# An attention kernel on one core: a transpose and a wait moved one slot on, and a pair of loads set apart

## The chip, the cores and the metric

One core of a Trainium2 chip. TensorE (PE) multiplies matrices, VectorE (DVE) and ScalarE (ACT) work on rows of 128 partitions, GpSimd (POOL) does the same more slowly, and SyncE (SP) here only issues transfers (DMAs). Each engine runs its own list of instructions in order, and semaphores join the lists. The metric is the time of one run on the device, in microseconds (us).

## What is computed

Two layers on 8 batches of 112 query rows and 375 context keys, all in float32, width 512. The first is an attention block with 16 heads of width 32 and an MLP. The second has two cross-attentions (called passes here) over the same context, each with 16 heads of width 128 and one learned extra key and value, and then an MLP:

```python
qh = (q_in @ wq + bq).reshape(b, q_len, H, K)
kh = (kv_in @ wk + bk).reshape(b, t, H, K)
vh = (kv_in @ wv + bv).reshape(b, t, H, K)
kh = jnp.concatenate([kh, bias_k], axis=1)   # broadcast over the batch
vh = jnp.concatenate([vh, bias_v], axis=1)
logits = jnp.einsum('bqhk,bthk->bhqt', qh, kh) / scale
weights = jax.nn.softmax(logits, axis=-1)
ctx = jnp.einsum('bhqt,bthk->bqhk', weights, vh).reshape(b, q_len, H * K)
x = res + ctx @ wo + bo
```

## The kernel before, in words

A float32 value is kept as two halves, high and low, and a product of two matrices is three matrix multiplications (high by high, high by low, low by high; `product`, L1877).

The two passes of the second layer take most of the run, and the change lies in them alone (`attend(a)` of each engine, a = 0 and 1). A pass works through 4 groups of 4 heads. For each group it walks over the 8 batches, so a pass has 32 places, each a (group, batch) pair. The batches of a group are called first to eighth below (`place.b` 0 to 7). Each place has 4 **slots**, t = 0 to 3, one for each head of its group. The place of a group is unrolled, and every engine's list is written by the same loop over places and slots, so that the order of the work is fixed by the code.

What the slots of a place hold, engine by engine:

- PE, in every slot: the keys of the head three ahead (`key`, 12 multiplications into `ps_k` or `ps_t`), then a part of the context sum of the place before (`context_sum`, 9 multiplications, probabilities `pt` by context `ckd`, into `ps_v` or `ps_o`), then the scores of the head two ahead (`scores`, 3 multiplications into `ps_s`). In the second and sixth batch (not in the second of a pass's first group) slots 2 and 3 hold no context sum but the output of two heads each for the four batches before (`head_output`, from `sums` and `w_b`); the place after takes twice the context sums in its slots 0 and 1.
- ACT: the high halves (`k_hi`, `sums_hi`), the exponentials (`prob`), and once a place, in slot 0, the high half of the turned probabilities (`pt_hi`, L1216).
- DVE: the low halves (`k_lo` L1642, `sums_lo` L1677), the maximum of each row (L1648), the scaling of the probabilities (L1536), and for each head one transposition of 32x32 squares (L1666) that writes the probabilities into the one buffer `blocks`.
- POOL: the low half of the turned probabilities (`pt_lo`, L944, three products of 1.3 us) in slot 1.
- SP issues, in this order: in slot 0 the context halves `cs_hi` and `cs_lo` of the place two ahead (`load_halves`, L641), when the keys of this place are done; in slot 1 the queries `q` of the place two ahead (L691), when this place's last scores are done; in slot 2 the store of `blocks` to the DRAM tensor `turned_probabilities` (L750), when all four heads of the place are in it; in slot 3 its load back as `pt_lo` in four pieces (L760), when the store has landed. Between them stand the loads of `ckd` (L651), and in the fourth and fifth batch of groups two to four the weights of the next group (`w_raw_a`, `w_raw_b`, 1 MB a batch). All are on one queue, SP's.

Since DVE works two heads ahead, the first head of a place is turned in slot 2 of the place before, and has to wait there until the store of `blocks` (L750) has read the buffer and landed (`blocks_out`, L1665). The turned probabilities then go store, load, `pt_hi`, `pt_lo`, and are used by PE in slot 2 of the next place (of the first and fifth batch: two places on).

Of the kernel before, what the change touches and what calls it, by code (L numbers as in the profile page):

```python
# [190 lines left out]
def build(nc, x_in, ctx_in, kd_in_all, mask_in, blocks_a, blocks_b, vec_a, vec_b, value_rows, value_bias_rows, row_bias, eye, out):  # L191
# [7 lines left out]
    with ExitStack() as ctx:  # L199
# [401 lines left out]
        def _(sp):  # L601
# [36 lines left out]
                    dst = ctx_scr[ds(place.b, 1), s].rearrange("o p f -> (o p) f")  # L638
                    sp.dma_start(dst, cs[place.parity][s][:, 0:DT * KW].bitcast(F32)).then_inc(ctx_out[place.parity], 16)

            def load_halves(place):  # L641

                for s in range(2):
                    src = ctx_scr[ds(place.b, 1), s].rearrange("o p f -> (o p) f")
                    sp.dma_start(cs[place.parity][s][:, 0:DT * KW].bitcast(F32), src).then_inc(ct_in[place.parity], 16)

# [76 lines left out]
            def attend(a):  # L723
                def store_head(place, t):
                    sp.wait_ge(z_ev, NT * place.quads + t + 1)
                    sp.sem_inc(sp_waited, 1)
                    b0 = place.b - place.quarter
                    dst = o_scr[place.group, b0:b0 + 4, :, t * LQ:(t + 1) * LQ].rearrange("b p r -> p b r")
                    sp.dma_start(dst, o_head[t % 2]).then_inc(z_out[t % 2], 16)

                def store_extra(place):
                    sp.wait_ge(extra_ev, NT * place.visit + NT)
                    sp.sem_inc(sp_waited, 1)
                    dst = pex_scr[ds(place.block, 1), ds(place.b, 1)].rearrange("o b (r t) -> r (o b t)", t=NT)
                    sp.dma_start(dst, extra_p[:, NT * place.parity:NT * place.parity + NT]).then_inc(extra_out[place.parity], 16)

                def load_extra(place):
                    first = place.quarter - 2
                    for i in range(2):
                        sp.wait_ge(extra_out[i], 16 * (place.pairs + first))  # L740
                    wait(sp, z_term, NT * place.quads)
                    sp.sem_inc(sp_waited, 1)
                    src = pex_scr[ds(place.block, 1), ds(place.b - 2 + first, 2)].rearrange("o b f -> o (b f)")
                    sp.dma_start(extra[:, 2 * first * NT * P:(2 * first + 2) * NT * P],
                                 src.partition_broadcast(P)).then_inc(extra_in, 16)

                def store_blocks(place):
                    sp.wait_ge(block_turn, turned_heads(place, NT))
                    sp.sem_inc(sp_waited, 1)
                    sp.dma_start(turned_scr[place.parity], image(place)).then_inc(blocks_out, 16)  # L750

                def load_turned(place):
                    sp.wait_ge(blocks_out, 16 * turned_batches(place) + 16)
                    wait(sp, c_mm, NT * (place.visit - 1))
                    sp.sem_inc(sp_waited, 1)
                    src = turned_scr[place.parity].rearrange("(i a) (s f) -> s a i f", i=BANDS, s=4)
                    for s in range(4):
                        rows = slice(SQUARE * s, SQUARE * (s + 1))
                        dst = pt[place.parity][1][rows, :].bitcast(F32).rearrange("a (i f) -> a i f", i=BANDS)
                        sp.dma_start(dst, src[s]).then_inc(turned_in[place.parity], 16)  # L760

                def q_stored(group):
                    for i in range(4):
                        sp.wait_ge(q_out[i], 16 * stores_before(i, 1, a, group))
                    sp.sem_inc(sp_waited, 1)

                def prologue(place):
                    def between(i):
                        if i == 0:
                            q_stored(1)  # L770
                            load_q(place)
                            load_q(place.next())

                    last_query(query, a, between, FIRST_PIECES)

                def all_queries_stored():
                    for i in range(4):
                        sp.wait_ge(q_out[i], 16 * stores_before(i, 1, a + 1, 0))
                    sp.sem_inc(sp_waited, 1)

                def one_batch(place):
                    for t in range(NT):
                        if t == 0 and place.after(2):
                            sp.wait_ge(k_mm, place.tile + NT)
                            sp.sem_inc(sp_waited, 1)
                            load_halves(place.after(2))
                        if t == 0 and place.final:
                            sp.wait_ge(k_mm, place.tile)
                            land(0, a, (0, 1))
                        if t == 1 and place.after(2):  # L790
                            load_q(place.after(2))
                        if t == 2:
                            store_extra(place)
                            if not place.final:
                                store_blocks(place)
                        if t == 3:
                            if not place.final:
                                load_turned(place)
                            if place.quarter >= 2:
                                load_extra(place)  # L800
                        for head in heads(place, t):
                            store_head(quad_before(place), head)
                        for summed, d in chunks(place, t):
                            load_by_key(summed.next(), d)
                        if query_piece(place, t):
                            last_query(query, a, skip, query_piece(place, t))
                        if place.fetches is not None:
                            load_block(place.fetches, (place.block_a, place.block_b)[place.fetches] + 1, [t])
                    if place.head and place.parity == 0:
                        all_queries_stored()  # L810

                def epilogue(place):
                    sp.wait_ge(k_mm, place.tile + NT)
                    sp.sem_inc(sp_waited, 1)
                    land(0, a, (2,))
                    load_block(0, place.block_a + 2)
                    for t in range(NT):
                        store_head(place, t)

                batches(sp, a, prologue, one_batch, epilogue)  # L820
# [574 lines left out]
        def _(dve):  # L1395
# [243 lines left out]
            def attend(a):  # L1639
# [11 lines left out]
                def normalized_1(place, t):  # L1651
# [6 lines left out]
                                          ALU.mult).then_inc(extra_ev, 1)  # L1658

                    normalize(place.unit + t, prob[buf], buf, extra_probability, slice(0, P))  # L1660
                    if place.final:
                        return
                    dve.wait_ge(s_norm, place.unit + t + 1)
                    if t == 0:
                        wait(dve, blocks_out, 16 * (turned_batches(place) - (place.head and place.parity)))  # L1665
# [24 lines left out]
                def prologue(place):  # L1690
                    def between(t):
                        if t == 0:
                            split_q(place)
                            key_lo(place, 0)
                            key_lo(place, 1)
                            maximum(place, 0)
                        if t == 1:
                            normalized_1(place, 0)
                            key_lo(place, 2)
                            maximum(place, 1)  # L1700
                            normalized_1(place, 1)

                    last_query(query, a, between, FIRST_PIECES)

                def one_batch(place):
                    for t in range(NT):
# [3 lines left out]
                            key_lo(*place.key(t + 3))  # L1710
                        for head in heads(place, t)[1:2]:
                            output(quad_before(place), head)
                        if place.final:
                            for summed, d in chunks(place, t):
                                sum_lo(summed, d)
# [8 lines left out]
                        for summed, d in () if place.final else chunks(place, t)[-1:]:  # L1724
                            sum_lo(summed, d)
                        if place.key(t + 2):
                            normalized_1(*place.key(t + 2))
                        if query_piece(place, t):
                            last_query(query, a, skip, query_piece(place, t))
                        if t == 0 and not place.final:  # L1730
# [145 lines left out]
        def _(pe):  # L1876
# [180 lines left out]
            def attend(a):  # L2057
# [55 lines left out]
                def one_batch(place):  # L2113
                    for t in range(NT):
                        for head in heads(place, t)[0:1]:
                            head_output(quad_before(place), head)
                        if t == 2 and not place.final:
                            pe.wait_ge(q_lo, place.batch + 2)
                        if place.key(t + 3):
                            key(*place.key(t + 3))  # L2120
                        for head in heads(place, t)[1:2]:
# [2 lines left out]
                            last_query(query, a, skip, query_piece(place, t))  # L2124
                        if t > 1 and query_piece(place, 3):
                            last_piece(place, t)
                        for summed, d in chunks(place, t):
                            context_sum(summed, d)
                            if place.final and t == 2 and d < 2:
                                last_turned(place, d + 2)  # L2130
# [151 lines left out]
```

## Time and profile before

| | |
|---|---|
| median of 3 runs | 2285.13 us (2279.72 to 2288.86) |
| the profiled execution's own time | 2283.49 us |
| its span, first to last instruction | 2281.6 us, granted PE clock 0.998 |
| PE busy | 2222.9 us (97%), 12347 matrix multiplications |
| DVE, ACT, POOL busy | 60%, 49%, 28% |
| SP's queue | 477.7 MB, 65.9% of 16 DMA engines' span |

The page says that PE is nearly always busy, so a change can win at most the little idle time that PE has, and can lose as much as it makes PE wait. In a row of the time line, the bracket at the end gives the engine's idle time just before the instruction, and what ended it. The window view gives, for each engine, busy time and number of instructions, and then the granted clock of PE, the share of time in which the DMA engines were busy, and what they moved.

### The profile page before, as it was taken

How to read it: one execution, taken by the hardware profiler on the slowest of the kernel's cores; microseconds unless marked ns; L12 is line 12 of the kernel's file. 1: busy time of each engine (PE TensorE's matmuls, PEld its weight loads, DVE VectorE, ACT ScalarE, POOL GpSimd, SP SyncE). 2: the span in 40 equal slices, each digit the busy share in tenths (PEclk: the TensorE clock that was granted, in tenths of full speed). 3: DMA queues.
4: the chain of work that ended last, by engine and by line, in shares of the span. 5: the costliest groups of instructions: out<-in, count | busy, mean ns of one | idle time of the engine just before them, and what ended most of it. 6: DMA issues, size and time to landing. Idle time of an engine off the chain costs nothing.

```text
span 2281.6 us, 36274 instructions
## 1 busy us (share of the span) xinstructions
PE 2222.9 (97%) x12347; PEld 2005.4 (88%) x12347; DVE 1376.4 (60%) x3070; ACT 1120.4 (49%) x2282; POOL 647.0 (28%) x945
## 2 busy tenths in 40 slices
PE   7999999999999999999999999999999999999999
PEld 6777788888999899899888898999899899888888
DVE  6877774524666666666654616666666566554743
ACT  5777753344455454455453434555455455453421
POOL 2111055421232332232322212233233133133421
PEclk9999999999999999999999999999999999999999
DMA  5422136566988888988975557987988988864110
GB/s 190 147 91 104 57 100 201 171 234 193 293 255 280 276 272 258 285 271 260 299 217 151 200 170 239 291 271 243 293 273 254 277 282 262 269 211 137 52 54 33
DMA packets 327767, 480.04 MB, mean 210 GB/s; under 512 B 65822, under 2 KB 250034, under 8 KB 327586
## 3 DMA queue, kind: packets, MB, share of 16 engines
q1 hardware_dynamic: 327586, 477.73, 65.9%
q8 instruction: 101, 1.65, 0.3%
q14 instruction: 80, 0.66, 0.1%
HBM read 368.72 MB, written 108.92 MB: 209 GB/s over the span
## 4 chain that ended last, share of the span: by engine, by line
PE 78%; DMA 8%; DVE 5%; issue 3%; SPq 3%; ACT 2%; POOL 1%; DVEq 0%; ACTq 0%; POOLq 0%
PE ps_o L1880 7%; PE ps_o L1882 7%; PE ps_o L1881 7%; PE ps_v L1880 5%; PE ps_k L1880 5%; PE ps_k L1881 5%; PE ps_k L1882 5%; PE ps_v L1882 5%; PE ps_v L1881 5%; DMA turned_probabilities<-blocks 5%; PE ps_t L1881 4%; PE ps_t L1882 4%; PE ps_t L1880 4%; PE ps_s L1880 4%; PE ps_s L1882 3%; PE ps_s L1881 3%
## 5 line engine op out<-in xcount | busy, mean ns | idle before, releaser
L944 POOL TENSOR_TENSOR pt_lo<-pt_lo,pt_hi 128x512 fp32r<-128x512 f32 x186 | 243.1, 1334 | 201.0 <-ACT pt_hi L1216 201.0
L1251 ACT ACTIVATE prob<-ps_s,row_columns 128x376 f32<-128x376 f32 x256 | 147.1, 575 | 249.9 <-DVE row_columns L1648 248.1
L937 POOL CAST k_hi<-xk_hi 128x1 fp32r<-128x1 f32 x256 | 53.0, 207 | 680.3 <-PE ps_s L1882 680.2
L1666 DVE STREAM_TRANSPOSE blocks<-prob 128x384 f32<-128x384 f32 x240 | 138.8, 579 | 148.0 <-DMA turned_probabilities<-blocks 141.2
L1880 PE MATMUL ps_k<-cs_hi,w_a_hi 128*128 128x376 f32 x636 | 217.8, 342 | 0.0
L1881 PE MATMUL ps_k<-cs_lo,w_a_hi 128*128 128x376 f32 x636 | 213.0, 335 | 0.0
L1882 PE MATMUL ps_k<-cs_hi,w_a_lo 128*128 128x376 f32 x636 | 211.7, 333 | 0.0
L1536 DVE TENSOR_SCALAR prob<-prob,row_columns 128x375 f32<-128x375 f32 (+1 forms) x384 | 204.6, 533 | 4.5
L892 POOL TENSOR_TENSOR w_b_lo<-w_raw_b,w_b_hi 128x512 fp32r<-128x512 f32 x80 | 108.5, 1381 | 332.7 <-ACT w_b_hi L996 332.7
L1648 DVE TENSOR_REDUCE row_columns<-ps_s 128x1 f32<-128x376 f32 x256 | 139.0, 543 | 95.5 <-PE ps_s L1882 95.3
L1880 PE MATMUL ps_t<-cs_hi,w_a_hi 128*128 128x376 f32 x512 | 172.1, 336 | 7.5 <-DVE q L1529 7.5
L1881 PE MATMUL ps_t<-cs_lo,w_a_hi 128*128 128x376 f32 x512 | 171.8, 336 | 0.0
L1882 PE MATMUL ps_t<-cs_hi,w_a_lo 128*128 128x376 f32 x512 | 171.4, 335 | 0.0
L1880 PE MATMUL ps_v<-pt_hi,ckd 128*128 128x448 f32 (+1 forms) x384 | 145.9, 380 | 9.1 <-POOL pt_lo L944 8.0
L892 POOL TENSOR_TENSOR w_a_lo<-w_raw_a,w_a_hi 128x512 fp32r<-128x512 f32 x76 | 100.6, 1342 | 183.2 <-ACT w_a_hi L996 183.2
L1882 PE MATMUL ps_v<-pt_hi,ckd 128*128 128x448 f32 (+1 forms) x384 | 142.7, 372 | 0.0
L1882 PE MATMUL ps_o<-pt_hi,ckd 128*128 128x448 f32 (+1 forms) x384 | 142.5, 371 | 0.0
L1880 PE MATMUL ps_o<-pt_hi,ckd 128*128 128x448 f32 (+1 forms) x384 | 142.1, 370 | 0.0
L1881 PE MATMUL ps_v<-pt_lo,ckd 128*128 128x448 f32 (+1 forms) x384 | 142.1, 370 | 0.0
L1881 PE MATMUL ps_o<-pt_lo,ckd 128*128 128x448 f32 (+1 forms) x384 | 141.4, 368 | 0.0
L1229 ACT ACTIVATE sums_hi<-ps_v 128x448 fp32r<-128x448 f32 x128 | 69.7, 545 | 131.1 <-PE ps_v L1882 130.9
L1229 ACT ACTIVATE sums_hi<-ps_o 128x448 fp32r<-128x448 f32 x128 | 69.5, 543 | 106.5 <-PE ps_o L1882 106.2
(291 smaller groups left out, 6288.7 us busy)
## 6 DMA issues: line engine op xcount, KB each, us to landing
ckd<-context_by_key_halves SPq DMA_DIRECT2D x256, 384.0 KB, 6.2
cs_hi<-context_halves SPq DMA_DIRECT2D x64, 752.0 KB, 7.1
cs_lo<-context_halves SPq DMA_DIRECT2D x64, 752.0 KB, 8.6
pt_lo<-turned_probabilities SPq DMA_DIRECT2D x248, 192.0 KB, 3.7
turned_probabilities<-blocks SPq DMA_DIRECT2D x60, 768.0 KB, 5.4
w_raw_b<-in_blocks_b SPq DMA_DIRECT2D x104, 256.0 KB, 3.8
w_raw_a<-in_blocks_a SPq DMA_DIRECT2D x104, 256.0 KB, 5.2
q<-q_scratch SPq DMA_DIRECT2D x64, 256.0 KB, 5.4
```

Source lines behind the costliest of these rows:

```text
L892: pool.tensor_tensor(w[slot][1][:, :, part], w_raw[slot][:, :, part], w[slot][0][:, :, part], ALU.subtract).then_inc(w_lo[slot], 1)
L937: pool.tensor_copy(k[t % 2][0][:, LK:KW], xk[0][:, ds(col, 1)])
L944: pool.tensor_tensor(lo, lo.bitcast(F32), hi, ALU.subtract).then_inc(t_lo, 1)
L1229: act.activation(sums[0][:, d, place.quarter * HALF:(place.quarter + 1) * HALF], ps_c[d % 2][:, 0:HALF], ACT.Identity).then_inc(c_hi, 1)
L1251: act.activation(prob[buf][:, 0:KW], ps_s[buf][:, 0:KW], ACT.Exp, bias=max_neg[:, buf:buf + 1], accum_out=prob_sum[:, buf:buf + 1]).then_i ...
L1536: dve.tensor_scalar(p[rows, 0:LK], p[rows, 0:LK], prob_rcp[rows, col:col + 1], None, ALU.mult).then_inc(s_norm, 1)
L1648: dve.tensor_reduce(max_neg[:, t % 2:t % 2 + 1], ps_s[t % 2][:, 0:KW], AX_X, ALU.max, negate=True).then_inc(s_max, 1)
L1666: dve.transpose(image(place).rearrange("p (s j t e) -> p t j s e", s=4, j=3, t=NT)[:, t], prob[buf][:, 0:BLOCKS * SQUARE].rearrange("p (j ...
L1880: pe.matmul(out, w_h, m_h, start=first, stop=False)
L1881: pe.matmul(out, w_h, m_l, start=False, stop=False)
L1882: return pe.matmul(out, w_l, m_h, start=False, stop=last)
```

## The change

Three things move; no computation is added or taken away.

1. On DVE the transposition gets a function of its own, `squares`. For the first head of a place it is called one slot later, in slot 3 of the place before, behind the low half of a key. For the other heads it stays where it was.
2. On SP only the high half of the context (`cs_hi`) is loaded in slot 0; the low half (`cs_lo`) follows in slot 1, behind the queries.
3. On PE the wait for the next place's queries (`q_lo`) in slot 2 is put behind the keys of that slot.

```diff
-            def load_halves(place):
+            def load_halves(place, halves=range(2)):
-                for s in range(2):
+                for s in halves:
...
-                            load_halves(place.after(2))
+                            load_halves(place.after(2), (0,))
...
                         if t == 1 and place.after(2):
                             load_q(place.after(2))
+                            load_halves(place.after(2), (1,))
...
                     normalize(place.unit + t, prob[buf], buf, extra_probability, slice(0, P))
-                    if place.final:
-                        return
+
+                def squares(place, t):
+                    buf = t % 2
                     dve.wait_ge(s_norm, place.unit + t + 1)
...
+                        if t == 3 and not place.final and not place.next().final:
+                            squares(place.next(), 0)
...
-                            normalized_1(*place.key(t + 2))
+                            following, head = place.key(t + 2)
+                            normalized_1(following, head)
+                            if head and not following.final:
+                                squares(following, head)
...
-                        if t == 2 and not place.final:
-                            pe.wait_ge(q_lo, place.batch + 2)
                         if place.key(t + 3):
                             key(*place.key(t + 3))
...
+                        if t == 2 and not place.final:
+                            pe.wait_ge(q_lo, place.batch + 2)
                         for summed, d in chunks(place, t):
```

SP's list in the third batch of a group, from the context halves to the load of the turned probabilities, before:

```order
L645 DMA cs_hi<-context_halves 128x1504
L645 DMA cs_lo<-context_halves 128x1504
L651 DMA ckd<-context_by_key_halves 128x768 x2
L691 DMA q<-q_scratch 128x4x128
L651 DMA ckd<-context_by_key_halves 128x768 x2
L735 DMA extra_probability<-extra_p 128x4
L750 DMA turned_probabilities<-blocks 128x1536
L651 DMA ckd<-context_by_key_halves 128x768
L760 DMA pt_lo<-turned_probabilities 32x4x384 x4
```

and in the changed kernel:

```order
L645 DMA cs_hi<-context_halves 128x1504
L651 DMA ckd<-context_by_key_halves 128x768 x2
L691 DMA q<-q_scratch 128x4x128
L645 DMA cs_lo<-context_halves 128x1504
L651 DMA ckd<-context_by_key_halves 128x768 x2
L735 DMA extra_probability<-extra_p 128x4
L750 DMA turned_probabilities<-blocks 128x1536
L651 DMA ckd<-context_by_key_halves 128x768
L760 DMA pt_lo<-turned_probabilities 32x4x384 x4
```

The low half now stands behind the queries, and so nearer to the store L750. Two loads of `ckd` have changed sides with it.

DVE's list at the end of slot 2 and in slot 3 of an ordinary place, with the semaphores that each instruction waits for, before:

```order
L1533 RECIPROCAL row_columns<-row_columns 128x1 [waits s_exp]
L1657 TENSOR_SCALAR extra_p<-prob,row_columns 128x1 [waits extra_out1,s_rcp]
L1536 TENSOR_SCALAR prob<-prob,row_columns 128x375
L1666 STREAM_TRANSPOSE blocks<-prob 128x3x4x32 [waits blocks_out,s_norm]
L1642 SCALAR_TENSOR_TENSOR k_lo<-ps_k,col_b,k_hi 128x375 [waits k_hi]
L1648 TENSOR_REDUCE row_columns<-ps_s 128x1 [waits s_mm]
L1677 TENSOR_TENSOR sums_lo<-ps_o,sums_hi 128x448 [waits c_hi]
```

and in the changed kernel:

```order
L1534 RECIPROCAL row_columns<-row_columns 128x1 [waits s_exp]
L1658 TENSOR_SCALAR extra_p<-prob,row_columns 128x1 [waits extra_out1,s_rcp]
L1537 TENSOR_SCALAR prob<-prob,row_columns 128x375
L1643 SCALAR_TENSOR_TENSOR k_lo<-ps_k,col_b,k_hi 128x375 [waits k_hi]
L1668 STREAM_TRANSPOSE blocks<-prob 128x3x4x32 [waits blocks_out,s_norm]
L1649 TENSOR_REDUCE row_columns<-ps_s 128x1 [waits s_mm]
L1679 TENSOR_TENSOR sums_lo<-ps_o,sums_hi 128x448 [waits c_hi]
```

The transposition that waits for the store and the low half of the key have changed places; what follows is as it was.

## Rows read from the trace of the kernel before

**Rows 1.** The page: the span; transfers of `cs_lo` (count, size each, median us to landing).

```profile
span 2281.6 us, 36274 instructions
...
cs_lo<-context_halves SPq DMA_DIRECT2D x64, 752.0 KB, 8.6
```

**Rows 2.** Waits of the whole run: who for whom, us in total, times, longest.

```profile
DVE blocks L1666 <- DMA turned_probabilities<-blocks: 141.2, 44, 6.7
...
PE ps_o L1880 <- DVE sums_lo L1677: 10.0, 6, 2.2
PE ps_v L1880 <- POOL pt_lo L944: 8.0, 22, 1.7
PE ps_t L1880 <- DVE q L1529: 7.5, 8, 1.8
PE ps_s L1880 <- DVE k_lo L1642: 5.5, 6, 1.5
```

**Rows 3.** Time line of SP, third batch of the third group: start, duration, what.

```profile
902.41 0.34 SPq L645 DMA_DIRECT2D cs_hi<-context_halves  x1
902.80 0.43 SPq L645 DMA_DIRECT2D cs_lo<-context_halves  x1
...
912.91 0.37 SPq L691 DMA_DIRECT2D q<-q_scratch  x1
...
915.64 0.32 SPq L750 DMA_DIRECT2D turned_probabilities<-blocks  x1
...
921.76 2.12 SPq L760 DMA_DIRECT2D pt_lo<-turned_probabilities  x4
```

**Rows 4.** Windows: after the engines come PE clock, DMA share, GB/s.

```profile
910.50:913.50 3.00, 3.00 (x17) 2.83 (x17) 1.21 (x3) 1.09 (x2) 3.00 (x4) 1.00 0.00 0
914.00:921.00 7.00, 7.00 (x39) 6.69 (x38) 3.67 (x10) 3.46 (x9) 1.80 (x2) 1.00 0.97 309
944.00:962.50 18.50, 17.36 (x92) 16.13 (x93) 11.66 (x27) 8.69 (x18) 5.08 (x11) 1.00 1.02 320
1808.70:1811.70 3.00, 3.00 (x11) 2.87 (x10) 1.26 (x3) 0.79 (x2) 0.11 (x1) 0.50 1.03 354
```

**Rows 5.** Tiles `cs_hi`, then `cs_lo`, window 902.3:903.2: from issue to landing.

```profile
DMA to landing us min/median/max: 4.4/4.4/4.4
...
DMA to landing us min/median/max: 5.9/5.9/5.9
```

**Rows 6.** Time line, eighth batches of two groups: ACT, POOL, PE's third product.

```profile
1014.62 1.49 ACT L1216 ACTIVATE pt_hi<-pt_lo 128x1536 fp32r<-128x1536 f32 x1 [0.70 <-DMA pt_lo<-turned_probabilities]
...
1016.18 3.80 POOL L944 TENSOR_TENSOR pt_lo<-pt_lo,pt_hi 128x512 fp32r<-128x512 f32 x3 [3.09 <-ACT pt_hi L1216]
...
1020.19 0.38 PE L1880 MATMUL ps_v<-pt_hi,ckd 119*128 119x448 f32 x1
...
1850.47 4.09 POOL L944 TENSOR_TENSOR pt_lo<-pt_lo,pt_hi 128x512 fp32r<-128x512 f32 x3 [2.33 <-ACT pt_hi L1216]
...
1855.23 0.38 PE L1880 MATMUL ps_v<-pt_hi,ckd 119*128 119x448 f32 x1
```

**Rows 7.** Time line, fifth and sixth batch of two groups: DVE, PE, ACT, PE.

```profile
963.61 0.58 DVE L1666 STREAM_TRANSPOSE blocks<-prob 128x384 f32<-128x384 f32 x1 [6.32 <-DMA turned_probabilities<-blocks]
...
964.74 0.44 PE L1880 MATMUL ps_s<-k_hi,q 128*128 128x376 f32 x1 [1.14 <-DVE k_lo L1642]
...
969.62 1.49 ACT L1216 ACTIVATE pt_hi<-pt_lo 128x1536 fp32r<-128x1536 f32 x1 [0.76 <-DMA pt_lo<-turned_probabilities]
...
973.26 0.47 PE L1880 MATMUL ps_o<-sums_hi,w_b_hi 128*128 128x448 f32 x1 [1.44 <-DVE sums_lo L1677]
...
1971.47 1.49 ACT L1216 ACTIVATE pt_hi<-pt_lo 128x1536 fp32r<-128x1536 f32 x1 [1.00 <-DMA pt_lo<-turned_probabilities]
...
1975.11 0.47 PE L1880 MATMUL ps_o<-sums_hi,w_b_hi 128*128 128x448 f32 x1 [1.68 <-DVE sums_lo L1677]
```

**Rows 8.** Time line of PE, sixth batch of the third group, pass two.

```profile
1806.76 0.48 PE L1880 MATMUL ps_o<-sums_hi,w_b_hi 128*128 128x448 f32 x1 [2.15 <-DVE sums_lo L1677]
```

More of the change, by code:

```diff
@@ L1698, in between @@
                             normalized_1(place, 0)
+                            squares(place, 0)
                             key_lo(place, 2)
@@ L1701, in between @@
                             normalized_1(place, 1)
+                            squares(place, 1)
                     last_query(query, a, between, FIRST_PIECES)
```

## The prediction

> **What bounds the kernel now.** I read the waits of the whole run first. The largest wait that the change touches is DVE's: 141.2 us in 44 waits for the store of `blocks` [rows 2]. But PE is the engine that is nearly always busy, so what counts is what PE waits for, and that is small: 10.0 us for `sums_lo`, 8.0 for `pt_lo`, 7.5 for `q`, 5.5 for `k_lo` [rows 2], 31.0 us together of a span of 2281.6 [rows 1]. That is the most that the change can win. The reader is to see that three of these four look like DVE being late, and DVE is late when it stands at that store.
>
> So I asked next what the store itself waits for, in the windows. Between the fourth and fifth batch of a later group (window 944 to 962.5), where 1 MB of weights is loaded as well, the DMA engines are busy without a gap, share 1.02, at 320 GB/s [rows 4]. There the queue sets the pace: the store of `blocks` stands at the end of what was issued before it. In the third batch it is otherwise: for 3.0 us, from 910.5 to 913.5, the share is 0.00, and from 914 to 921 it is 0.97 [rows 4]. SP's time line says why: `cs_hi` and `cs_lo` go out at 902.41 and 902.80, and then comes nothing that matters until PE's scores release `q` at 912.91; the store follows at 915.64, and `pt_lo` is asked for at 921.76, when the store has landed [rows 3]. `cs_hi` lands 4.4 us after its issue and `cs_lo` 5.9 us after its own, 0.39 us later [rows 3, 5]. So they land one behind the other, 5.9 + 0.39 - 4.4 = 1.9 us apart.
>
> Last, the time line at the two places where PE meets that chain. In the eighth batch (third group) ACT starts `pt_hi` at 1014.62, the moment `pt_lo` lands; POOL ends its third product at 1016.18 + 3.80 = 1019.98, and PE takes it at 1020.19 [rows 6]. PE had 0.21 us to spare. In the sixth batch PE stands still until 973.26, and ACT's `pt_hi`, released by the landing of `pt_lo`, began at 969.62: 3.64 us earlier [rows 7]. The same pair in the last of six such places is 1971.47 and 1975.11, again 3.64 [rows 7]. ACT makes `pt_hi` before `k_hi` and `sums_hi`, DVE's `sums_lo` follows, and PE's head output needs it. So PE's wait at `sums_lo`, though put down to DVE, begins with the landing of `pt_lo`.
>
> **The change part by part.**
>
> *The transposition one slot later.* Nothing is added: as many transpositions, 240 of them. At 963.61 DVE had stood 6.32 us; the low half of a key was behind it, and PE waited 1.14 us for that at 964.74 [rows 7]. In the changed kernel the key comes first, so this wait goes: all `k_lo` waits together are 5.5 us [rows 2]. What is late next is the wait of 1.44 us at 973.26, 8.5 us later in the same batch [rows 7]. It hangs on the landing of `pt_lo`, not on DVE, so PE gets there earlier and waits by as much longer. Bounds: -5.5 if the time stays won, 0 if it is only moved; I take 0, since the rows of the first and last such place give the same 3.64. Behind the transposition the maximum and the scaling of the next head wait as before.
>
> *The wait for `q` behind the keys.* PE's 12 key products hide it, so up to 7.5 us of waits go [rows 2]. In the same slot PE next needs `pt_lo`, for which it waits 8.0 us as it is [rows 2]. Bounds -7.5 and 0; I take 0 on the same ground: the third product cannot start before POOL's third.
>
> *The low half behind `q`.* It counts 752 KB [rows 1] and 1.9 us of the queue. Where the queue never runs dry, its place does not matter: the same bytes stand before the store. In the third batch of groups two to four and the seventh of groups one to three, in both passes, twelve times, the queue was dry before `q` was issued: those batches have twice the context sums in slots 0 and 1, so `q` is released late, as in the row above. There the low half was free, because it used time in which nothing else was there to carry. Now it goes out at about 913.4, with the loads of `ckd`, in front of the store of 915.64, into the window that is 0.97 busy [rows 3, 4]. The store, and the load behind it, land 1.9 us later. Bounds: 0 if the store passes it, 752 KB at 309 GB/s = 2.5 us if it runs at the mean of that window; I take 1.9, which is the measured distance of the same two loads.
>
> What this costs PE, by place:
> - Third to sixth batch, six times: the queue stays busy from the third batch's store to the landing of `pt_lo` in the sixth, so all 1.9 us arrive, and PE goes on 3.64 us after that landing: 6 x 1.9 = 11.4 us.
> - Eighth batch, six times: 1.9 us less the spare time. That is 0.21 us in the place above, and in the loosest 1855.23 - (1850.47 + 4.09) = 0.67 [rows 6]. This makes 1.2 to 1.7; the next batch asks for some of the rest again. I take 1.6: 9.6 us.
> - The clock. In the sixth batch of the third group, second pass, PE stood 2.15 us at one instruction [rows 8]. From 1808.7 to 1811.7 its granted clock was 0.50, the lower level of 1.2 GHz, so that those 3.0 us held work for 1.5 [rows 4]. The other five waits there are shorter (1.44 and 1.68 in the two shown [rows 7]), and the mean clock stayed high. When the `k_lo` wait moves into this one, and 1.14 + 1.44 = 2.6 us stand at one instruction, I expect the fall in those five too: 5 x 1.5 = 7.5 us. Bounds 0 and 9 (six).
>
> Sum: 11.4 + 9.6 + 7.5 = 28.5 us. The profiled execution took 2283.5 us, 1.6 below the median of three, so the changed kernel should take 2283.5 + 28.5 = 2312 us.
>
> Two rules of the Trainium skill bear on the low half. "DMA: Bandwidth & Descriptors", section "Two DMAs through the same engine are not ordered", says that nothing orders transfers across the 16 engines; read so, the store could land as early as before, and the sum would be near 0. Here the two halves, issued 0.39 us apart, landed 1.9 us apart [rows 3, 5], and the section "Queues, rings and completion order" of that page also has each engine take its ring in order, which is what these rows look like. "Perfetto Trace Analysis", section "DMA Optimizations", says that splitting transfers may let some start sooner if the DMA engines are generally idle. That speaks for setting the halves apart; with a share of 1.02 and 0.97 [rows 4] they are not idle, and the rule does not reach this place.
>
> **The rivals.**
>
> *No change (0.18).* The store lands as before, because the transfers overlap in the queue more than the halves did, and the released DVE and `q` waits turn into waits for `pt_lo`. For it: waits of DVE mostly cost PE nothing (141.2 us against 31.0 [rows 2]). Against it: the 1.9 us, and the full windows. It gives 2283.5 us, 2277 to 2291.
>
> *Faster (0.12).* The four pieces of `pt_lo` land sooner, because the low half no longer stands 0.4 us behind the high one while they are under way, and the chain that I hold fixed moves up. It would have to win back more than the 1.9 us that the store loses; from that point DVE and `q` decide, and the waits of rows 2 go. Gone entirely: 2283.5 - 31.0 = 2252.5; without those of `pt_lo`: 2283.5 - 23.0 = 2260.5, which I take. Against it: the low half is issued behind these pieces and the halves land in order of issue.
>
> *Worse (0.12).* The clock falls in the eighth batch and at `pt_lo` in the fifth too, where waits of 0.6 to 0.7 us now come three in a row: twelve more places at 1.5 us = 18, so 2330 us. For it: the level of 0.50 after one stop [rows 4, 8]. Against it: each stop there is short, with products between.
>
> **How the numbers follow.** The forecast has 0.58, with a range of its own from 2300 (no clock loss and some of the delay hidden: 2283.5 + 11.4 + 6) to 2320 (2.5 us instead of 1.9). No measurement of this kernel tells less than about 0.5% (11.4 us) from no change. The range goes from 2281, which leaves out the faster case and the lower part of no change, to 2324, which leaves out most of the worse one. Faster by over 0.5%: 0.12. Slower: 0.58 + 0.12, less 0.02 for the forecast's lower end = 0.68. Within: 0.20.
>
> **What would show it.** In the window 910.5 to 913.5 of the third batch the share stays 0.00 and begins earlier, and the store takes about 8 us to land instead of 6. PE's waits for `k_lo` and `q` nearly vanish; those for `pt_lo` (8.0) grow past 20 and those for `sums_lo` (10.0) to about 25. The distance of 3.64 us stays. The clock shows 0.50 after the sixth batch's stop in six groups. I am wrong if the store's time to landing is unchanged in the third and seventh batch, or if PE goes on less than 3.6 us after ACT's `pt_hi` begins.

## The result, and the profile after

The changed kernel took 2330.14 us (median of four runs, 2328.2 to 2340.3), the kernel before, beside it, 2283.09 (2279.72 to 2288.86). The ratio is 1.0213, with a 95% interval from 1.0189 to 1.0237: 47 us slower. The direction was predicted, the size was not: 2312 us was forecast, and the range ended at 2324. The profiled execution took 2340.3 us, the slowest of its four, so its sums run a little high.

First the waits that the prediction named, of the changed kernel (columns as in [rows 2]), and the page's row of `cs_lo`, which answers to [rows 1].

```profile
DVE blocks L1668 <- DMA turned_probabilities<-blocks: 127.0, 42, 5.4
...
PE ps_v L1889 <- POOL pt_lo L945: 38.1, 67, 3.9
...
PE ps_o L1889 <- DVE sums_lo L1679: 25.1, 12, 4.2
```

```profile
span 2338.4 us, 36336 instructions
...
cs_lo<-context_halves SPq DMA_DIRECT2D x64, 752.0 KB, 7.0
```

PE's waits for `k_lo` and `q` in the attention, 13.0 us in [rows 2], have no row any more. Those for `pt_lo` went from 8.0 to 38.1 us and those for `sums_lo` from 10.0 to 25.1. DVE waits 14 us less at the store of `blocks`, and the low half lands 7.0 us after its issue instead of 8.6: both parts of the change do what they say, and PE has no wait for `cs_lo`, so the low half is not late for its keys. The kernel is slower all the same. An engine's shorter wait is no gain when PE did not hang on it.

Next the time line of SP in the third batch of the third group, and the windows of the same stretch (after the engines: PE clock, DMA share, GB/s). They answer to [rows 3] and [rows 4].

```profile
922.59 0.34 SPq L645 DMA_DIRECT2D cs_hi<-context_halves  x1
...
933.09 0.37 SPq L691 DMA_DIRECT2D q<-q_scratch  x1
933.51 0.50 SPq L645 DMA_DIRECT2D cs_lo<-context_halves  x1
...
935.82 0.42 SPq L750 DMA_DIRECT2D turned_probabilities<-blocks  x1
...
944.31 1.74 SPq L760 DMA_DIRECT2D pt_lo<-turned_probabilities  x4
```

```profile
929.50:934.00 4.50, 4.50 (x25) 4.24 (x24) 2.54 (x5) 1.78 (x4) 4.39 (x5) 1.00 0.00 1
934.00:945.00 11.00, 11.00 (x61) 10.58 (x60) 5.14 (x14) 4.18 (x10) 2.81 (x4) 1.00 0.88 275
994.10:997.40 3.30, 2.67 (x8) 2.54 (x9) 3.03 (x7) 1.77 (x3) 2.68 (x4) 0.50 1.08 382
```

The queue stands dry for 4.5 us, and behind that the low half goes out in front of the store. SP asks for `pt_lo` 944.31 - 935.82 = 8.5 us after the store's issue, where it was 6.1 in [rows 3]. That is 2.4 us longer, not the 1.9 that I had put on it.

Then what PE meets, in the same group: the second batch (PE), the sixth (ACT, PE) and the eighth (ACT, POOL, PE). They answer to [rows 6] and [rows 7].

```profile
907.00 0.47 PE L1889 MATMUL ps_o<-sums_hi,w_b_hi 128*128 128x448 f32 x1 [1.75 <-DVE sums_lo L1679]
...
991.11 1.48 ACT L1217 ACTIVATE pt_hi<-pt_lo 128x1536 fp32r<-128x1536 f32 x1 [1.03 <-DMA pt_lo<-turned_probabilities]
...
994.73 0.74 PE L1889 MATMUL ps_o<-sums_hi,w_b_hi 128*128 128x448 f32 x1 [3.04 <-DVE sums_lo L1679]
...
1041.51 1.49 ACT L1217 ACTIVATE pt_hi<-pt_lo 128x1536 fp32r<-128x1536 f32 x1 [1.99 <-DMA pt_lo<-turned_probabilities]
...
1043.07 3.75 POOL L945 TENSOR_TENSOR pt_lo<-pt_lo,pt_hi 128x512 fp32r<-128x512 f32 x3 [4.17 <-ACT pt_hi L1217]
...
1044.49 0.45 PE L1889 MATMUL ps_v<-pt_hi,ckd 128*128 128x448 f32 x1 [1.15 <-POOL pt_lo L945]
```

In the sixth batch PE goes on 994.73 - 991.11 = 3.62 us after ACT's `pt_hi` begins, as before (3.64). It now stands 3.04 us at one instruction, and behind it the granted clock is 0.50, the lower level of 1.2 GHz (third window above). In the eighth batch, where it had 0.21 us to spare, it stands 1.15 us at POOL's first product. The stop in the second batch, 1.75 us at `sums_lo`, was in no step of the prediction.

### The profile page after: what moved, and what is told of

Its sections match the earlier page's. It is cut to its first block, busy times and chain, and to the rows that moved or that the text cites. A ratio compares the mean times of both kernels' runs of the same rounds, so it can differ in the third digit from the quotient of the medians.

```text
span 2338.4 us, 36336 instructions
## 1 busy us (share of the span) xinstructions
PE 2246.3 (96%) x12347; PEld 2017.4 (86%) x12347; DVE 1379.9 (59%) x3070; ACT 1117.4 (48%) x2282; POOL 646.5 (28%) x945
## 4 chain that ended last, share of the span: by engine, by line
PE 64%; DMA 16%; DVE 8%; issue 5%; ACT 3%; SPq 2%; POOL 2%; ACTq 0%; DVEq 0%; POOLq 0%
DMA turned_probabilities<-blocks 10%; PE ps_o L1889 6%; PE ps_o L1891 6%; PE ps_o L1890 6%; DMA pt_lo<-turned_probabilities 5%; PE ps_v L1889 4%; PE ps_k L1889 4%; PE ps_k L1890 4%; PE ps_v L1891 4%; PE ps_k L1891 4%; PE ps_v L1890 4%; PE ps_s L1889 3%; PE ps_s L1891 3%; PE ps_s L1890 3%; PE ps_t L1890 3%
## 5 line engine op out<-in xcount | busy, mean ns | idle before, releaser
L1889 PE MATMUL ps_v<-pt_hi,ckd 128*128 128x448 f32 (+1 forms) x384 | 150.9, 393 | 39.2 <-POOL pt_lo L945 38.1
L1643 DVE SCALAR_TENSOR_TENSOR k_lo<-ps_k,col_b,k_hi 128x375 fp32r<-128x375 f32 x128 | 77.6, 606 | 131.7 <-ACT k_hi L1212 131.7
L1891 PE MATMUL ps_v<-pt_hi,ckd 128*128 128x448 f32 (+1 forms) x384 | 143.7, 374 | 0.0
L1889 PEld LDWEIGHTS ps_v<-pt_hi,ckd 128*128 128x128 f32 (+1 forms) x384 | 72.5, 189 | 70.3 <-POOL pt_lo L945 34.8
```

Of the source, the lines that this page charges most:

```text
L1643: dve.scalar_tensor_tensor(out=k[t % 2][1][:, 0:LK], in0=key_bank(place, t)[:, 0:LK], scalar=col_b[:, ds(place.column((C_BK0, C_BK1), t), 1)],
L1889: pe.matmul(out, w_h, m_h, start=first, stop=False)
L1891: return pe.matmul(out, w_l, m_h, start=False, stop=last)
```

## The experiments

Each series of runs had the kernel before beside it on the same chip. Its median was 2276.6, 2286.2, 2278.6 and 2275.9 us in the four series, so ratios are compared. What the clock takes is estimated as (1 - mean granted clock of the runs) x time, as if all of it fell on work that PE had to do. It is 4.3 to 5.5 us for the kernel before (0.9976 to 0.9981) and 20 us for the changed one (0.9912).

### Which part of the change costs

**The low half alone** (`split_only`), on the kernel before:

```
-    load_halves(place.after(2))          # slot 0
+    load_halves(place.after(2), (0,))    # slot 0
     load_q(place.after(2))               # slot 1
+    load_halves(place.after(2), (1,))
```

> The kernel before with one edit: in every batch the low half is issued behind q. Transpositions and the wait for q stay as before. Theory (the low half alone delays the store of the blocks and what hangs on it): about 2330 us, 2318 to 2342, that is at least 35 of the 47 us; PE waits at pt_lo and sums_lo together over 40 us (before 18.0), and the third batch's store takes 8 us or more to land. Rival (the moved transposition or the moved wait for q carries a good part): below 2306 us. Both could add: if the moves help by what they removed (13 us of waits), this run is slower than the changed kernel, about 2340.

Ratio 1.0193 (1.0174 to 1.0213), +45 us. The waits at `pt_lo` and `sums_lo` are 15.6 and 13.6 us, 29 together and not over 40; those for `q` rose from 7.5 to 16.4. A chain that ends later shows at whichever instruction PE meets first, and with the wait for `q` still ahead of the keys, that is `q`. The mean clock was 0.996, so by the estimate the clock takes 9.3 us, 5 more than before: some 40 of the 45 us are delay at full clock.

**The two moves alone** (`moves_only`): the changed kernel with `load_halves(place.after(2))` in slot 0 again.

> The changed kernel with the two halves together in slot 0 again; the transposition and the wait for q are moved as in the changed kernel. Theory (the moved waits are taken over by the chain of pt_lo): 2283 us, within 6. Rival one (the transposition one slot on hurts by itself): over 2295 us. Rival two (the waits for k_lo and q that went, 13.0 us, are really won, and the low half costs 60 instead of 47): about 2270 us.

Ratio 1.0060 (1.0039 to 1.0080), +13.7 us, beyond the 6 that I gave it. The rows below are PE in the sixth batch of the second group, pass two, the window behind it, and PE's two waits of the whole run.

```profile
1640.03 0.47 PE L1888 MATMUL ps_o<-sums_hi,w_b_hi 128*128 128x448 f32 x1 [3.36 <-DVE sums_lo L1678]
```

```profile
1641.50:1644.70 3.20, 3.20 (x11) 3.13 (x10) 1.51 (x3) 0.39 (x1) 0.58 (x3) 0.50 1.09 373
```

```profile
PE ps_o L1888 <- DVE sums_lo L1678: 19.2, 6, 3.5
PE ps_v L1888 <- POOL pt_lo L944: 13.5, 22, 3.4
```

The two rows grew by 9.2 + 5.5 = 14.7 us, which is what left the rows of `k_lo` and `q` (13.0) and a little more. So the waits were handed on, as predicted. But they were handed on into one long stop each, and the clock falls: the mean of the five runs is 0.9928, by the estimate 16.5 us against some 4.3 in that series' kernel before. That difference of 12 is nearly the whole of the 13.7. The clock did not fall at every such stop. Five of the six sixth batches show 0.50; in the fourth group of pass two, below, PE stood as long and went on at 1.00:

```profile
1977.58 0.48 PE L1888 MATMUL ps_o<-sums_hi,w_b_hi 128*128 128x448 f32 x1 [3.32 <-DVE sums_lo L1678]
```

```profile
1977.60:1981.00 3.40, 3.40 (x19) 3.29 (x20) 2.80 (x5) 1.51 (x4) 2.04 (x4) 1.00 1.04 365
```

**Each move by itself** (`transposition_only` and `q_wait_only`).

```
 transposition_only:                       q_wait_only:
     normalized_1(place, t)                -    pe.wait_ge(q_lo, place.batch + 2)
-    transpose at once                          key(*place.key(t + 3))
+    transpose one slot on (squares)            output of the second head
                                           +    pe.wait_ge(q_lo, place.batch + 2)
```

> The kernel before, with the transposition one slot later alone; halves together and the wait for q where it was. In the run with both moves and the halves together the time rose by 0.6% while the mean granted clock fell from 0.998 to 0.993, with five of six sixth batches at 0.50 for 3.41 us behind one stop of 2.85 to 3.66 us. Theory (the wait for k_lo goes and the wait for sums_lo grows by as much, so that one stop is long enough for the clock to fall): 4 to 5 more such stretches than before, each costing 1.7 us, so 7 to 9 us or 0.3 to 0.4% above before. Rival one (the wait for q does it): within 3 us of before. Rival two (the store of the blocks is issued later, and the time is lost at full clock): above before by 6 us or more with the clock at 0.998.

> The kernel before, with PE's wait for q behind the key products alone. Theory (the stop at q joins the stop at pt_lo behind it, where both stand in one slot: the start of each pass and the fifth batches): the q waits of 7.5 us go, those for pt_lo rise from 8.0 to about 14, and 1 to 3 more stretches at 0.50 make it 2 to 5 us slower (0.1 to 0.2%). Rival (the wait is hidden behind the keys and won): 5 to 7 us faster.

The transposition: 1.0029 (1.0017 to 1.0041), 6.6 us; the mean clock of ten runs is 0.9949 against 0.9978, by the estimate 6.6 us as well. The profiled run had five stretches at 0.50 in the attention, two more than before rather than four or five, one of them twice as long. PE and the window behind it, sixth batch of the third group, pass two:

```profile
1812.01 0.47 PE L1888 MATMUL ps_o<-sums_hi,w_b_hi 128*128 128x448 f32 x1 [3.86 <-DVE sums_lo L1678]
```

```profile
1812.70:1816.00 3.30, 3.30 (x12) 3.25 (x12) 2.28 (x3) 0.53 (x1) 1.35 (x3) 0.50 1.05 358
```

The wait for `q`: 1.0000 (0.9988 to 1.0012). Its waits went, and those for `pt_lo` rose from 8.0 to 17.6 us, where I had expected 14. The mean clock fell too (0.9958), by the estimate 4.6 us, and neither that loss nor the gain of the rival is in the time. Whether something was won back is not shown; the estimate from the clock can be wrong by this much.

### Where the low half costs

**Only in the third and seventh batch** (`split_at_outputs`), **only in the others** (`split_elsewhere`), and **the changed kernel with the halves joined there** (`after_joined`).

```
 split_at_outputs, on the kernel before:
-    load_halves(place.after(2))
+    load_halves(place.after(2), (0,) if place.quarter == 2 else range(2))
     load_q(place.after(2))
+    if place.quarter == 2: load_halves(place.after(2), (1,))
 split_elsewhere: the same with != 2
 after_joined, on the changed kernel: both halves in slot 0 if place.quarter == 2
```

> The kernel before, with the low half issued behind q in the third and the seventh batch of each group only (16 of 64 batches); elsewhere both halves stay together. Theory (the place of the low half matters only where the queue had run dry): 35 us or more of the 47, so 2318 us or more. Rival (it costs the same in every batch): 16/64 of 47 = 12 us, so 2295 us.

> The kernel before, with the low half behind q in every batch but the third and the seventh of each group. The prediction put this at nothing: where the queue is never dry, the same bytes stand in front of the store. Theory now (other batches have dry moments too, above all the first batch of a group): 4 to 11 us above before (0.2 to 0.5%), since the split in all batches cost 45 us and in the third and seventh alone 33. Rival (the prediction was right on this, and the 12 us between those two runs are spread of the measurement): within 3 us of before.

> The changed kernel, with both halves together in slot 0 in the third and seventh batch of each group; apart in all others. Theory (the parts add up: 13 us from the moves, 45 - 33 = 12 us from the split in the other batches): 20 to 28 us above before (0.9 to 1.2%), and the eighth batches have no stop over 0.5 us. Rival (with the moves, the split hurts in every batch): 35 us or more above before.

They gave 1.0140 (1.0115 to 1.0164), 1.0056 (1.0042 to 1.0070) and 1.0082 (1.0066 to 1.0098): +32, +13 and +19 us. So 16 of 64 batches carry 1.40 of the 1.93% of the split, and they carry it in the changed kernel too (2.13 - 0.82 = 1.3%). The first fell short of the 35 that I expected, since the other 48 batches are not free. The last fell short too: I expected at least 20, the sum of the moves (0.60%) and the other batches (0.56%), and 0.82% came. The transfer of the store (`turned_probabilities`), third batch of the third group: tile rows of the kernel before, then of `split_at_outputs`, and the latter's window from the low half to the store's landing.

```profile
DMA to landing us min/median/max: 6.0/6.0/6.0
```

```profile
DMA to landing us min/median/max: 8.4/8.4/8.4
```

```profile
918.50:928.60 10.10, 10.10 (x56) 9.75 (x56) 3.73 (x11) 4.06 (x10) 2.81 (x4) 1.00 0.96 295
```

Over the six third and the six seventh batches that the prediction counted, the mean from issue to landing went from 5.9 to 8.45 and from 5.8 to 8.2 us: 2.5 us. At the 295 GB/s of this window, 752 KB (128 x 1504 x 4 = 770,048 bytes) take 2.6. The 1.9 us of the prediction came from a faster stretch. In the kernel before, `cs_hi` landed at 906.8 and `cs_lo` at 908.7, and between the two the engines moved 402 GB/s, at which the same bytes take 1.9:

```profile
906.80:908.70 1.90, 1.90 (x13) 1.88 (x12) 1.63 (x6) 1.86 (x4) 0.24 (x2) 1.00 1.01 402
```

**The same distance, but ahead of the wait** (`lo_before_q`):

```
     load_halves(place.after(2), (0,))    # slot 0
+    load_halves(place.after(2), (1,))    # slot 1
     load_q(place.after(2))
```

> The kernel before, with the low half issued in slot 1 directly in front of the load of q instead of behind it; both halves are still apart by a slot. In the third and seventh batch the load of q waits for PE's scores, so that here the low half goes out before that wait, while the queue is dry, and in the split kernel after it. Theory (the low half costs because it is behind the wait for q and so in front of the store at the busy time): no more than 6 us above before (0.25%), the third batch's store lands about 6 us after its issue. Rival (setting the two halves apart costs by itself, for instance because each alone leaves the queue unevenly loaded): 30 us or more above before, as with the low half behind q (+45).

Ratio 1.0001 (0.9984 to 1.0017). Two neighbouring lines change places and 45 us are gone. SP in the third batch of the third group:

```profile
906.13 0.43 SPq L645 DMA_DIRECT2D cs_lo<-context_halves  x1
912.52 0.37 SPq L691 DMA_DIRECT2D q<-q_scratch  x1
...
915.25 0.32 SPq L750 DMA_DIRECT2D turned_probabilities<-blocks  x1
...
921.50 0.80 SPq L760 DMA_DIRECT2D pt_lo<-turned_probabilities  x2
```

The low half is out at 906.13, 6.4 us ahead of `q`, and SP asks for `pt_lo` 6.25 us after the store's issue, so the store has landed by then. Setting the halves apart costs nothing; being behind SP's wait for PE's scores does.

**What is left in the other batches** (`split_busy`: fourth to sixth batch, `split_first`: first batch; the same edit with another condition).

> The kernel before, with the low half behind q in the fourth, fifth and sixth batch of each group only, where the queue has no gap. The split in all batches but the third and seventh cost 0.56% (13 us), where the prediction said nothing. Theory one (the prediction was right for a queue without a gap, and the 13 us come from the first, second and eighth batches, whose stores land about 1 us later): within 4 us of before (0.17%). Theory two (the place of the low half matters in a full queue too): 6 us or more above before, half of the 13.

> The kernel before, with the low half behind q in the first batch of each group only (8 of 64). Theory one (the first batch's store lands 1 us later, and PE pays for it in the second batch, at sums_lo, where 4 us of new stops stood): 3 to 6 us above before (0.15 to 0.25%). Theory two (an even price over 48 batches): 2 us, not to be told from none.

The fourth to sixth batch: 1.0015 (1.0005 to 1.0026), 3.4 us in 24 batches. The first: 1.0035 (1.0022 to 1.0048), 8 us in 8 batches, more than the 3 to 6 that I expected. The two make 0.50 of the 0.56%, so little is left for the second and eighth batches, which had no run of their own. In the traces the first batch's store takes 6.4 us to land instead of 5.2 (means of eight), and PE meets that in the second batch. The row is PE in the second batch of the fourth group of `split_first`:

```profile
1057.77 0.48 PE L1882 MATMUL ps_o<-sums_hi,w_b_hi 128*128 128x448 f32 x1 [1.27 <-DVE sums_lo L1679]
```

Why the first batch's store comes later, with a DMA share of 0.95 to 0.97 in both kernels, stays open.

### What brings time back

**The low half behind the store** (`behind_store`): `load_halves(place.after(2), (1,))` follows `store_blocks(place)` in slot 2.

> The kernel before, with the low half issued in slot 2 right behind the store of the blocks, in every batch. Theory (what counts is the bytes that stand in front of the store): the store lands about 1.9 us earlier in the batches with a busy queue, and the low half runs while the load of pt_lo still waits for the landing of the store: PE's waits for pt_lo and sums_lo (18.0 us) shrink to under 8, and the time is 2265 to 2276 us. Rival one (the load of pt_lo now stands behind the low half, so it lands as before): 2283 us, within 5. Rival two (the low half, needed by the first key some 10 us later, is late): over 2295 us, with new waits of the first key's products.

This went wrong: 1.0163 (1.0135 to 1.0191), +37 us, and PE's waits for `pt_lo` and `sums_lo` are 48.0 us instead of under 8. Rival one named the cause but had it cost nothing; of rival two there is little (2.6 us of waits for `cs_lo`). The pieces of `pt_lo` in the fourth batch of the third group, from issue to landing, first in the kernel before, then three of the four here:

```profile
DMA to landing us min/median/max: 2.9/3.7/4.3
```

```profile
DMA to landing us min/median/max: 5.2/5.6/6.4
```

The store itself lands sooner, 4.9 us after its issue instead of 8.0, but the low half is still in the queue when SP asks for `pt_lo`. From the issue of the store to the last landing of `pt_lo` it is 15.7 us in this batch instead of 13.7. In the means by batch, it is 1.1 to 1.7 us longer in six of the eight, 0.3 in the fifth and no longer in the eighth. So the low half delays the chain from behind the store too: by less than the 2.5 us, but in most batches.

**The products that fill the stop** (`after_keys_first` on the changed kernel, `keys_first` on the kernel before) and **later weights** (`weights_later`; `keys_first_weights` has both edits).

```
 keys_first, PE, slot 2 of an output batch:
-    head_output(..., 0)                  # 12 products, the last 3 wait for sums_lo
+    head_output(..., 0, range(DT - 1))
     key(*place.key(t + 3))               # 12 products
+    head_output(..., 0, (DT - 1,))
     head_output(..., 1)
 weights_later:
-    self.fetches = {3: 0, 4: 1}.get(self.b)
+    self.fetches = {3: 0, 5: 1}.get(self.b)
```

> The changed kernel, with PE's order altered in the output batches: the last three products of the first head's output, which wait for sums_lo, come behind the twelve products of the next key (2.06 us) instead of in front of them. Nothing else differs. Theory (in the sixth batches PE stands 3 to 4 us at sums_lo at one instruction, and this stop also lets the clock fall for 3.41 or 6.83 us): the stops shrink by about 2 us each in ten places or so, and most of the stretches at 0.50 behind them go: 20 to 30 us below the changed kernel, so 0.8 to 1.2% above before. Rival (the time lost at the stop is handed on to the next wait of the chain, as the prediction said of the waits for k_lo and q): 5 us below the changed kernel at most.

> The kernel before with the same altered order on PE and nothing else. Theory: the sums_lo waits of 10.0 us go, the fifth and sixth batches keep their k_lo, q and pt_lo waits: 6 to 12 us below before (0.3 to 0.5%). Rival (the chain hands it on): within 3 us.

> The kernel before, with the second 0.5 MB of weights of a group loaded in its sixth batch instead of its fifth. Theory (in the fourth to sixth batch what stands in front of the store sets PE's stops of 33.9 us): the fifth batch's store lands 1.5 to 2 us earlier in six groups, and the time is 8 to 14 us below before (0.35 to 0.6%). Rival (the queue's backlog reaches into the sixth and seventh batch and the bytes are only paid for later): within 4 us of before or slower, with new stops in the seventh and eighth batch.

> The kernel before, with the key's products ahead of the wait for sums_lo and the second weights in the sixth batch: the two edits that each made it faster, 0.61% and 0.68%. If they take away different stops, they add up to 1.2 to 1.3% (27 to 29 us); if both take away the same sixth-batch stops, 0.8 to 1.0%.

`after_keys_first` gave 1.0111 (1.0089 to 1.0134): 1.0% below the changed kernel by the order of three products. PE's waits in it:

```profile
PE ps_v L1889 <- POOL pt_lo L945: 36.0, 58, 6.4
...
PE ps_o L1889 <- DVE sums_lo L1679: 7.3, 6, 2.3
```

The waits for `sums_lo` fell from 25.1 to 7.3 us and the mean clock rose from 0.9912 to 0.9942; `pt_lo` kept its 36. On the kernel before the same edit gave 0.9939 (0.9925 to 0.9953), 14 us; `weights_later` gave 0.9932 (0.9917 to 0.9948), 15 us. Each is a little more than I expected of it. In `weights_later` the fifth batch's store lands 6.5 us after its issue instead of 7.8 (means of six groups). What moved there is 1 MB, four loads of 256 KB, and not the 0.5 MB that I wrote in the expectation. Both together gave 0.9914 (0.9899 to 0.9929): 2256.4 against 2275.9 us, faster than both kernels of this case. That is two thirds of the sum of the two. Both take away the same stops: the output's waits for `sums_lo`, 10.0 us in [rows 2], have no row in `keys_first` and are 3.2 us in `weights_later`.

## Why the direction was right and the size wrong

Three terms of the sum failed. The delay of the low half was taken as 1.9 us and was 2.5; its price in the other batches was put at nothing and was 13 us; and the clock was charged 7.5 us, where by the estimate it took some 15.

- **What costs.** Right: the low half, by its place in front of the store where the queue had been dry. `lo_before_q` and `split_at_outputs` show it.
- **The 1.9 us.** Mis-sized. The store came 2.5 us later, which was the upper bound (752 KB at the rate of the busy window). I took the distance of the two landings, from a stretch that ran at 402 GB/s; the delay follows the rate of the stretch that the bytes move into, 295 GB/s. In the trace of `split_at_outputs`, against an undisturbed batch, the six eighth batches lost 12.8 us (0.4 before; I had 9.6) and the fourth to sixth of six groups 43.3 (33.9 before, 29.4 in `lo_before_q`; I had 11.4 more). By its time this part cost 32 us where I had 21.0, and 21.0 x 2.5 / 1.9 = 27.6. So the size of the delay explains most of that gap, not all. Some of the rest is in two places outside my twelve: in the third batch of each pass's first group the store landed after 5.3 and 6.0 us instead of 4.4 and 4.2, and the fourth batch took 0.7 and 1.3 us longer. The sums from traces are of one execution each (that of `split_at_outputs` was the fastest of its four), and they differ by some us from run to run, as the 33.9 and the 29.4 do.
- **"Where the queue never runs dry, its place does not matter."** This step failed in its reach. It nearly holds where I looked, in the fourth to sixth batch (3.4 us in 24 batches). I extended it unread to the first batches, which cost 8 us, and the second batch's stop at `sums_lo` follows from them. All batches but the third and seventh cost 13 us where I had none.
- **The moved waits.** Right that they would be handed on: `k_lo` and `q` lost 13.0 us, and `moves_only` shows 14.7 more at `sums_lo` and `pt_lo`. The wait for `q` came out at zero, as forecast.
- **The clock.** The mechanism was as forecast, the price too low: a wait that joins another at one instruction can let the clock fall there. Five of six sixth batches show it, also with the halves together. I charged 5 x 1.5 = 7.5 us. In the profiled changed kernel the clock stayed at 0.50 for 3.4 us in two of the five and for 6.8 us in three, and two eighth batches and a fifth fell too. The starts of the passes fell as well, but they did so in the kernel before. By the estimate the moves alone lose 12 us more than the kernel before, the changed kernel some 15. The rival "worse" named the eighth and fifth batches and gave 2330 us. But it had the delay at 21 us and more falls than there were, so its number is right by two errors against each other.
- **The sum.** By batches the low half adds up: 1.40 (third and seventh) + 0.56 (the others) = 1.96%, against 1.93 for all. With the moves it does not: 1.93 + 0.60 (`moves_only`) = 2.53%, against 2.13 (1.89 to 2.37) measured. Taken singly the moves are 0.29 and 0.00, and with these it would be 2.22. In `after_joined` the parts come to 1.16 and the run to 0.82. Both gaps are little wider than the intervals allow; if they are real, some of what the moves cost and some of what the low half costs is the same loss, and how it divides is not shown.

Of the signs that I named, the store's 8 us, the dry window, the 3.64 us and the four waits came as described; `pt_lo` went well past the 20, and the clock fell in five of the six groups.

## What to carry to other kernels

Where one engine issues all transfers, look at what a moved transfer stands behind, not at how far it is from its use: the same load was free ahead of a wait and cost 2% behind it. Price its bytes at the rate of the stretch that they move into. And before a wait is merged with the next one, look at what the longer stop does to the clock, and look for independent products to put in front of it: here three products moved behind twelve others gave 0.6 to 1.0%.

## What the runs showed of the hardware

By the estimate from the mean clock, some 15 of the 47 us went with TensorE's clock, though PE was 96% busy and the mean clock 0.991. In the two windows at 0.50 shown of `moves_only` and `transposition_only` PE was busy without a gap, and yet only 11 and 12 products ran in 3.2 and 3.3 us; at 1.00, behind the stop of 3.32 us, 19 ran in 3.4. The length of one stop does not by itself tell whether the clock falls. Stops of 3.04, 3.36 and 3.86 us had a stretch at 0.50 at their end or behind them, and so had one of 2.15 us [rows 8]; with stops of 1.44 and 1.68 us in [rows 7] the clock stayed. But it also stayed with the one of 3.32 us, and in an eighth batch of the changed kernel it fell behind a stop of 1.04 us with two of 0.3 us after it. What decides between them stays open.
